# Second block in the wide order, shared sets mixed half in the first and half in the second block

## The reference

```python
xn = layernorm(x)                                   # no gain
s = silu(xn @ w_gate.T)                             # 2752 columns
idx = top_k(-abs(s), 1376)                          # per token: the smaller half by magnitude
s[idx] = 0
a = (s * (xn @ w_up.T)) @ w_down.T
h = relu(xn @ up_w) ** 2                            # 2048 columns
shared = h @ down_w
latent = xn @ fc1_w                                 # 512 columns
routed = (latent @ expert_w) * sum(top_k(xn @ gate_w, 2)) @ fc2_w
y = x + a + layernorm(shared + routed) * gamma + beta
```

## Time and profile before

| | |
|---|---|
| median of 3 runs | 2283.11 us (2279.87 to 2283.51) |
| the profiled execution | 2282.36 us, its span 2280.1 us |
| PE busy | 2263.9 us, 99% of the span, 10264 matmuls and transposes |
| VectorE (DVE) busy | 1327.3 us, 58% |
| GpSimd (POOL) busy | 939.2 us, 41% |
| ScalarE (ACT) busy | 751.3 us, 33% |
| granted TensorE clock | 1.00 over the span |
| DMA | 637.07 MB, mean 279 GB/s, engines busy 79.9% of the span |

### The profile page before, as it was taken

How to read it: one execution, slowest core, us unless ns; L and a number is a source line. 1 busy time by engine, 2 the same in 40 slices (tenths; PEclk the granted TensorE clock), 3 DMA queues, 4 the chain that set the end, 5 groups by cost and what they waited for, 6 DMA issues and landing times.

```text
span 2280.1 us, 27377 instructions
## 1 busy us (share of the span) xinstructions
PE 2263.9 (99%) x10264; PEld 1882.5 (83%) x10264; DVE 1327.3 (58%) x1712; ACT 751.3 (33%) x1173; POOL 939.2 (41%) x670
## 2 busy tenths in 40 slices
PE   8999999999999999999999999999999999999999
PEld 6888888888888888888888888888788888888877
DVE  4332678757334456937434446788943543888870
ACT  3233654133334325301114334623112432551310
POOL 5456557487444523044014461136403455043620
PEclk9999999999999999999999999999999999999999
DMA  6799999788888878887678887668677888676955
GB/s 257 278 389 395 354 366 354 264 341 299 292 297 280 273 278 312 295 292 289 213 233 296 272 278 284 213 228 288 239 251 248 268 283 309 216 231 226 333 186 177
DMA packets 229158, 637.07 MB, mean 279 GB/s; under 512 B 23712, under 2 KB 32928, under 8 KB 225952
## 3 DMA queue, kind: packets, MB, share of 16 engines
q1 hardware_dynamic: 229024, 635.30, 79.9%
HBM read 483.10 MB, written 152.11 MB: 279 GB/s over the span
## 4 chain that ended last, share of the span: by engine, by line
PE 92%; DVE 3%; DMA 2%; SPq 1%; POOL 1%; ACT 1%; issue 0%; DVEq 0%; ACTq 0%
PE bank L1330 30%; PE bank L1332 30%; PE bank L1331 30%; PE bank L1350 1%; DMA mixed_w<-mixes 1%; DVE prod L1925 1%; DMA split_w<-w 1%; PE bank L1341 1%; SPq L800 0%; POOL w L1061 0%; SPq L796 0%; DVE prod_t L2061 0%; DVEq L1491 0%; PE bank L1430 0%; PE bank L1431 0%
## 5 line engine op out<-in xcount | busy, mean ns | idle before, releaser
L1061 POOL TENSOR_TENSOR w<-raw,w 128x512 fp32r<-128x512 f32 (+1 forms) x196 | 282.3, 1447 | 195.0 <-ACT w L1107 194.6
L1066 POOL TENSOR_TENSOR w<-w 128x512 fp32r<-128x512 f32 x146 | 214.5, 1496 | 199.1 <-ACT w L1284 199.0
L1330 PE MATMUL bank<-w,prod_t 128*128 128x512 f32 x672 | 269.5, 401 | 3.0 <-DVE prod_t L2061 3.0
L1332 PE MATMUL bank<-w,prod_t 128*128 128x512 f32 x672 | 262.9, 391 | 0.0
L1331 PE MATMUL bank<-w,prod_t 128*128 128x512 f32 x672 | 261.9, 390 | 0.0
L1330 PE MATMUL bank<-w,tok 128*128 128x512 f32 (+1 forms) x664 | 252.8, 381 | 0.7 <-ACT mag L1218 0.5
L1331 PE MATMUL bank<-w,tok 128*128 128x512 f32 (+1 forms) x664 | 252.0, 380 | 0.0
L1332 PE MATMUL bank<-w,tok 128*128 128x512 f32 (+1 forms) x664 | 252.0, 379 | 0.0
L1330 PE MATMUL bank<-tok,w 128*128 128x512 f32 x640 | 249.0, 389 | 0.0
L1331 PE MATMUL bank<-tok,w 128*128 128x512 f32 x640 | 249.0, 389 | 0.0
L1332 PE MATMUL bank<-tok,w 128*128 128x512 f32 x640 | 249.0, 389 | 0.0
(11 more groups left out here) (222 smaller groups left out, 4633.7 us busy)
## 6 DMA issues: line engine op xcount, KB each, us to landing
w<-split_w SPq DMA_DIRECT2D x448, 512.0 KB, 4.5
split_w<-w SPq DMA_DIRECT2D x184, 512.0 KB, 6.2
w<-mixed_w SPq DMA_DIRECT2D x176, 256.0 KB, 3.2
w_more<-split_w SPq DMA_DIRECT2D x88, 512.0 KB, 5.1
w_more<-mixed_w SPq DMA_DIRECT2D x128, 256.0 KB, 3.7
rows<-x_dram SPq DMA_DIRECT2D x32, 512.0 KB, 5.0
mixed_w<-own SPq DMA_DIRECT2D x12, 1024.0 KB, 6.8
spilled_u<-prod SPq DMA_DIRECT2D x12, 1024.0 KB, 8.0
```

Source lines behind the costliest of these rows:

```text
L1061: pool.tensor_tensor(lo, words, hi, ALU.subtract).then_inc(lo_ready, 1)
L1066: pool.tensor_tensor(slot_of(g)[:, 1, :], slot_of(g)[:, 1, :].bitcast(F32), slot_of(g)[:, 0, :], ALU.subtract).then_inc(pool_lo, 1)
L1330: pe.matmul(out, left[0], right[0], start=first, stop=False)
L1332: return pe.matmul(out, left[1], right[0], start=False, stop=last)
```

## The change

`WIDE` becomes true for block 1, so its shared steps are computed as the pairs 5 and 6 in the wide order, 296 granules instead of 272. The sets that these pairs need are therefore mixed earlier. The four sets of pair 5 (`FIRST_SHARED`) are mixed in block 0, loaded from the granules 148, 158, 176 and 192, mixed seven and stored eight granules later, in a place of their own (`first_own`, over `below`); the first load waits for the first four masks. The four sets of pair 6 (`SECOND_SHARED`) are mixed in block 1, from the granules 149, 156, 163 and 170: two loads at each of two granules, the mix three and the store five behind, in `shared_own`. Two waits are added: the slots over `first_own` wait in block 1 for the first four stores, and ScalarE's `upper_early_sum` in block 1 for all eight, since it writes over `shared_own`. In all wide blocks the norms begin at out0+11 instead of out0+9 (three granules apart as before); the second token normalisation moves from out1+3 to out1+4, and the first two token loads from out0+18 and out0+21 to out0+20 and out1+1. The norm constants of block 1 are loaded where a wide block loads them, at 252. VectorE's operations for a set stay the same four.

```diff
--- before.py
+++ after.py
@@ -67,7 +67,7 @@
          (("shared", 0), ("shared", 1)), (("shared", 2), ("shared", 3))]
 
 FAST = [0, 5, 5, 5]
-WIDE = [False, False, True, True]
+WIDE = [False, True, True, True]
 SHARED_PAIRS = [5, 6]
 FIRST_PAIRS = 2
 UP_PAIR, SPILLED = 2, (3, 4)
@@ -262,12 +262,12 @@
         self.hidden_at = {end[("hidden", i)] + LAG + 1 + (1 if later and i > 1 else 2) * t: (i, t) for i in range(SC) for t in range(TILES)}
         if wide:
             self.read_hidden_at, self.hidden_at = {}, {}
-        self.norm_at = [out0 + (9 if wide else 6) + (3 if later else 5) * t for t in range(TILES)]
-        self.tokens_at = [out1 + 1, out1 + 3] if wide else [out0 + 20, out0 + 21] if later else [out1 + 2, out1 + 4]
+        self.norm_at = [out0 + (11 if wide else 6) + (3 if later else 5) * t for t in range(TILES)]
+        self.tokens_at = [out1 + 1, out1 + 4] if wide else [out0 + 20, out0 + 21] if later else [out1 + 2, out1 + 4]
         self.tokens_at += [out1 + 10, out1 + 14]
         self.turn_tokens_at = {out1 + TURN_AFTER[t] + LAG: t for t in range(TILES)}
         self.residual_load = [ups + 2, ups + 3, self.norm_at[0] + 3, self.norm_at[1] + 3]
-        self.tokens_load = [out0 + 18, out0 + 21] if wide else [out0 + 14, out0 + 15] if later else [self.norm_at[2] + 3, self.norm_at[3] + 3]
+        self.tokens_load = [out0 + 20, out1 + 1] if wide else [out0 + 14, out0 + 15] if later else [self.norm_at[2] + 3, self.norm_at[3] + 3]
         self.tokens_load += [out1 + 7, out1 + 11]
 
 
@@ -445,10 +445,12 @@
 
 
 SHARED_SETS = range(SHARED_PAIRS[0] * HALF, (SHARED_PAIRS[1] + 1) * HALF)
-SHARED_FROM = {n: 158 + 7 * i for i, n in enumerate(SHARED_SETS)}
-SHARED_LOADS = {at + i: (n, i) for n, at in SHARED_FROM.items() for i in range(4)}
-SHARED_AT = {at + 5: n for n, at in SHARED_FROM.items()}
-SHARED_STORES = {at + 6: n for n, at in SHARED_FROM.items()}
+FIRST_SHARED, SECOND_SHARED = SHARED_SETS[:HALF], SHARED_SETS[HALF:]
+SHARED_FROM = [dict(zip(FIRST_SHARED, (148, 158, 176, 192))), dict(zip(SECOND_SHARED, (149, 156, 163, 170)))]
+SHARED_LOADS = [{at + i: [(n, i)] for n, at in SHARED_FROM[0].items() for i in range(4)},
+                {at + i: [(n, 2 * i), (n, 2 * i + 1)] for n, at in SHARED_FROM[1].items() for i in range(2)}]
+SHARED_AT = [{at + 7: n for n, at in SHARED_FROM[0].items()}, {at + 3: n for n, at in SHARED_FROM[1].items()}]
+SHARED_STORES = [{at + 8: n for n, at in SHARED_FROM[0].items()}, {at + 5: n for n, at in SHARED_FROM[1].items()}]
 
 
 MIX_PLACE = [0, 3, 2, 1]
@@ -628,6 +630,7 @@
 
         w_more = over("w_more", [P, EXTRA, 2, N], F32R, more_at)
         own = over("own", [P, 4, N], F32, more_at)
+        first_own = over("first_own", [P, 4, N], F32, more_at + 2 * HID * 4)
         junk_at = nc.sbuf_base - GK * P * 4
         junk_v = over("junk_v", [P, GK, P], BF16, junk_at)
         junk_s = over("junk_s", [P, GK, P], U8, junk_at + GK * P * 2)
@@ -775,6 +778,10 @@
 
             return raw_more[:, i, :]
 
+        def shared_place(n):
+
+            return first_own if n in FIRST_SHARED else shared_own
+
         def results_of(name):
 
             kind, c = name
@@ -834,16 +841,18 @@
             def load_shared_mix(n, i):
 
                 p, k = n // HALF, n % HALF
-                if n > SHARED_SETS[0]:
+                if n == FIRST_SHARED[0]:
+                    sp.wait_ge(masked, TILES)
+                elif n != SECOND_SHARED[0]:
                     sp.wait_ge(shared_stored, 16 * (n - SHARED_SETS[0]))
                 else:
                     sp.wait_ge(bank_filled, filled(1, ("fast", FAST[1] - 1, len(PRODUCTS) - 1, 1)))
                 src, width = words_of((PAIRS[p][i // 2], k + i % 2 * HALF))
-                sp.dma_start(shared_own[:, i, :], src).then_inc(shared_loaded, 16)
+                sp.dma_start(shared_place(n)[:, i, :], src).then_inc(shared_loaded, 16)
 
             def store_shared_mix(n):
                 sp.wait_ge(shared_mixes, 4 * (n - SHARED_SETS[0]) + 4)
-                sp.dma_start(mixed_w[n].rearrange("i p n -> p i n"), shared_own[:, :, :]).then_inc(shared_stored, 16)
+                sp.dma_start(mixed_w[n].rearrange("i p n -> p i n"), shared_place(n)[:, :, :]).then_inc(shared_stored, 16)
 
             def load_norm(b):
 
@@ -868,6 +877,8 @@
                 slot_free(sp, g)
                 if SLOT[g] >= RING and m < PHASE[b, 0] + RING + EXTRA:
                     sp.wait_ge(apply_step, b * 4 * TILES)
+                    if b == 1:
+                        sp.wait_ge(shared_stored, 16 * len(FIRST_SHARED))
                 for n, p in enumerate(SHARED_PAIRS):
                     if WIDE[b] and SLOT[g] >= RING and m in range(PHASE[b, p], PHASE[b, p] + RING + EXTRA):
                         if n == 0:
@@ -929,10 +940,11 @@
                     load_own_mix(*OWN_LOADS[m])
                 if b == 0 and m in OWN_STORES:
                     store_own_mix(OWN_STORES[m])
-                if b == 1 and m in SHARED_LOADS:
-                    load_shared_mix(*SHARED_LOADS[m])
-                if b == 1 and m in SHARED_STORES:
-                    store_shared_mix(SHARED_STORES[m])
+                if b < 2:
+                    for n, i in SHARED_LOADS[b].get(m, []):
+                        load_shared_mix(n, i)
+                    if m in SHARED_STORES[b]:
+                        store_shared_mix(SHARED_STORES[b][m])
                 if m == (plan.norm_load if b else FIRST_NORM_LOAD):
                     load_norm(b)
                 if b:
@@ -1187,6 +1199,8 @@
             def upper_early_sum(b, n):
 
                 act.wait_ge(unit_summed, shared_round(b, n) * UNIT_SUMS + 1)
+                if b == 1 and n == 0:
+                    act.wait_ge(shared_stored, 16 * len(SHARED_SETS))
                 act.activation(unit_sums_r[:, SUM_SLOT["S3"][0], :, :], unit_sums[:, EARLY_RAW, :, :],
                                ACT.Copy).then_inc(unit_sum_hi, 1)
 
@@ -1565,7 +1579,7 @@
 
             def mix_shared(n):
 
-                b11, b21, b12, b22 = (shared_own[:, i, :] for i in range(4))
+                b11, b21, b12, b22 = (shared_place(n)[:, i, :] for i in range(4))
                 at = 4 * (n - SHARED_SETS[0])
                 dve.wait_ge(shared_loaded, 64 * (n - SHARED_SETS[0] + 1))
                 dve.tensor_tensor(b11, b12, b11, ALU.subtract).then_inc(shared_mixes, 1)
@@ -1989,8 +2003,8 @@
                         dve.wait_ge(mixed_hi, MIXED[g])
                         dve.tensor_tensor(slot_of(g)[:, 1, :], slot_of(g)[:, 1, :].bitcast(F32), slot_of(g)[:, 0, :],
                                           ALU.subtract).then_inc(vector_lo, 1)
-                    if b == 1 and m in SHARED_AT:
-                        mix_shared(SHARED_AT[m])
+                    if b < 2 and m in SHARED_AT[b]:
+                        mix_shared(SHARED_AT[b][m])
                     if m in plan.units_at:
                         make_units(b, *plan.units_at[m])
                     if m in plan.lower_at:
```

## The result

The changed kernel takes 2288.43 us, median of 15 runs (2284.73 to 2291.79), the kernel before 2281.75 beside it (15 runs, 2279.87 to 2286.73): ratio 1.0027, interval 1.002 to 1.0034. So it is slower by 4.6 to 7.8 us. The forecast was 2282.5, no change; the time lies inside its range, near the 2291 of rival (b). The profiled execution took 2288.73 us with a span of 2286.9, 6.8 more than the span before.

A forecast was written before the change was run, and what follows sets the result against it. PE, busy nearly the whole span, was taken as the bound: matmul and transpose count plus stalls. Terms +2.7 +0.1 -4.1 +0.6 = -0.7 on the profiled 2282.36 gave 2281.7, or 2282.5 as median; range 2273 to 2292.

The forecast's parts named there:

- rival (b): Whole kernel slower: second-block chain later than walked, stage stall 16, clock 2.2, first block 4, giving 2291 us; chance 0.19.
- The direct gain: Second block: 48 matmuls fewer, 10.9 us; priced whole by the third block as 8.2 us, 557.29 to 549.06.
- The norm shift: out0 of blocks 2 and 3: norms two granules later save 2.05 us in each, 4.1 in all.
- the mixes in the search: Second block, VectorE's search chain: mixes and their load waits delay PE's operands, a stall of 10.4 us.
- the stall of the stage: Second block, pair 5: PE stalls 10.4 us in total because VectorE's chain is late; bounds 7 and 16.
- the walk: Second block: VectorE's chain timed step by step from granule 148's start, putting A12 at 108.3 us, wanted at 97.9.
- Step 5: Second block, a search step in VectorE's chain, put at 88.8 us from granule 148's start.
- First block: +2.7: Block 0, granules 155 to 164: four more sets' loads and stores delay raw loads, costing 2.7 us; bounds 0.5 and 6.
- Sets 22 and 23: nothing: Block 0: these two sets cost nothing, falling where raw halves have 5 to 9 us of lead.
- Covered, by 1 us: Wide blocks: banks free by 1680.7, first token turned about 1681.9, so the later second token row costs nothing.
- rival (c): Norm shift does not pay: second token row late, stall moves from out0 to out1, 2288.6 us; chance 0.10.
- Clock: +0.6: Second block: stalls of 2 to 5 us may halve PE's clock once, costing 0.6 us; bounds 0 and 4.4.

The follow-up runs named there:

- two_places: Changed kernel with pair 6's sets in two alternating places, loaded ahead and mixed where VectorE stood idle; 2271.18 us, ratio 0.9957 to the kernel before.
- norms_only: Kernel before with only the out0 norms, token normalisations and token loads of the wide blocks moved; 2277.11 us, ratio 0.9985.
- places_only: Changed kernel with pair 6's sets in two alternating places, loads at 149, 152, 163, 168, mixes unmoved; 2281.15 us, ratio 0.9995 to the kernel before.
- first_mix_later: Changed kernel with the mix of set 24 at granule 157 instead of 152, still one place; 2287.43 us, ratio 1.0027 to the kernel before.
- sets_in_out1: Changed kernel with block 0's sets 22 and 23 loaded from 186 and 200, mixed at 195 and 207; 2293.18 us, ratio 1.0055 to the kernel before.
- no_mix_work: Changed kernel without VectorE's mix operations for sets 24 to 27, loads, stores and waits kept; 2284.57 us, ratio 1.0017 to the kernel before.
- combined: two_places with block 0's sets 22 and 23 loaded, mixed and stored later, second token row at out1; 2266.85 us, ratio 0.9938 to the kernel before.

## Why the prediction was wrong

**What was right.** The direct gain: the bare wide second block as 547.0 (546.9 in two_places). The norm shift as -4.1 (-4.0 in norms_only). That the mixes in the search turn the gain of the second block into a stall through VectorE, not through PE's or the memory's load; the first wait and the start of the chain up to 32 us within 0.4 us.

**The term that failed: the stall of the stage, 10.4 us, measured 16.9** (563.95 less 547.0). The step that failed is the walk's landing time of a store. It had mix 25 at 33.4, which leaves 5.0 us for the store of set 24, the median of the earlier trace rows. The store landed after 9.2 us, and mix 25 came 4.5 us late: 4.2 by the store, 0.3 by what was late before. places_only, which takes this wait away, gains 5.8. Step 5's slow operation adds 2.2, the walk had 1 us too much elsewhere, and the last 0.8 us lie behind A12 (PE began its product 0.65 us behind VectorE, the walk had it there at once). I took the median for a place where the queue holds two spills, and that choice turned the sign. In the seven kernels with the changed second block the store of set 24, issued among the spills, took 5.8 to 12.3 us; the eight stores of the kernel before took 5.0 to 5.9. That the spills are what slows it fits, but no run took them away.

Rival (b) came near in time, 2291, in part by luck. Its bound of 16 us for the stall stood on loads landing near 7.8 us and on a mix of 6.8. The loads of the sets 24 to 27 landed within 6.6 us in the kernel after, and the mixes there took 0.68 us an operation.

**Where PE stands.** The prediction named ScalarE's and VectorE's operands. The first wait (5.2) is for VectorE's units; the largest (6.2) is for GpSimd's half of the weights at granule 184. These slots lie over the search's scratch, SP may load them only when the last count is done (931.05), so they are late by the same chain. A price by A12 alone still came out right, since A12 was ready at the same moment. The other kernels bear it out: A12 was late against 97.1 by 16.9, 16.6, 16.3, 12.4 and 11.3 us (after, first_mix_later, sets_in_out1, no_mix_work, places_only), and block 1 was longer than 547.0 by 16.9, 16.5, 16.3, 12.3 and 11.1.

**First block: +2.7, measured 3.6, or 4.5 from granule 40 on.** Size inside the bounds, place wrong. The raw loads at 155 to 164 had no lateness. "Sets 22 and 23: nothing" was the wrong sentence: it weighed only SP's raw loads and not VectorE's queue, where set 22 stands ahead of halves of turned products that PE reads at once. It waits 3.9 us there and works 6.4, and sets_in_out1 and combined gave those 4.1 us back. Another 0.7 us at granule 174 stayed in both, and no run names their cause.

**Norm shift.** Right alone, -2.7 in the kernel after, because the second token row was late once. "Covered, by 1 us" was 0.7; rival (c) happened with 1.7 us of its 6.1, in one block.

**Clock: +0.6, measured about 0.** The clock did fall to half, twice, so the wait-then-slow mechanism was right, but both times PE had another wait ahead in the same stage. I had added the term to the stall, and it must be weighed against what is late next; this is worked out from the traces, for no run changes the clock alone. Where nothing is, it costs: in sets_in_out1 the wait of 4.1 us before granule 201 was the last of its stretch, the granted clock between 600 and 603 us was 0.70, and granule 201 took 4.44 us for 2.72. (Columns as in the earlier trace rows.)

```profile
598.00:600.00 2.00, 1.91 (x5) 1.57 (x6) 1.02 (x2) 2.00 (x5) 2.00 (x3) 0.60 1.05 417
600.00:603.00 3.00, 3.00 (x11) 2.30 (x11) 0.36 (x1) 0.17 (x1) 1.75 (x2) 0.70 1.03 400
```

**Sum.** -0.8 (head, not of the change) + 3.6 + 6.7 - 0.35 - 2.3 = +6.8 against the -0.7 worked out. The one mis-sized term, 6.5 us too low, is most of the 7.5 us between them. The Trainium skill (DMA: Bandwidth & Descriptors, Rules for kernel authors), issue early and wait late, agrees with two_places; but first_mix_later waited later and gained nothing, since with one place the load itself couldn't be issued early.

## What to carry to other kernels

A buffer that is loaded, worked on and stored in a round has a period of its own: price the round (load landing, wait for the engine, work, store landing at that place of the queue) before the work, and try a second place before you move the work. Put side work into the idle gaps that the timeline of the same stage already shows; there 10.8 us of it cost nothing, while ahead of queued work 4 operations cost 4 us. Where a store waits for a mix, list it well behind the mix, for what is queued behind it may be a row that three other engines wait for.

## What the runs showed of the hardware

- VectorE and GpSimd slow each other. Where GpSimd works on tensors as well, a mix operation takes 1.5 to 1.8 us instead of 0.69 (rows of set 22 above), and GpSimd's own operations in that stretch 1.73 instead of 1.29, both at the same pace of 1.7 us. The Trainium skill (SBUF — State Buffer, SBUF: two separate sides) has an exclusive lock on a port pair that the two share, one blocked while the other's operation runs; the equal pace agrees. By turns alone it would be 1.85 us, an estimate from their starts when each is alone (0.60 and 1.25 us apart); the measured 1.7 is a little less, and no run here explains that. GpSimd in the same stretch:

```profile
534.26 1.29 POOL L1073 TENSOR_TENSOR w<-raw,w 128x512 fp32r<-128x512 f32 x1
535.51 1.73 POOL L1104 TENSOR_TENSOR prod<-prod,mag 128x512 f32<-128x512 f32 x1
537.20 1.74 POOL L1073 TENSOR_TENSOR w<-raw,w 128x512 fp32r<-128x512 f32 x1
```

- The granted clock fell to its lower level (1.2 GHz) toward the end of PE's waits of 6.2 and 5.2 us and, in sets_in_out1, right behind the one of 4.1 us in mid-kernel. It stayed at 1.00 (2.4 GHz) behind the wait of 2.1 us before granule 168 in no_mix_work and behind those of 1.0 to 1.4 us in out0 of block 0.
- The landing of one and the same kind of store or load swings from kernel to kernel: 5.8, 9.2 and 12.3 us for the 1 MB store of set 24 among the spills in three kernels, 4.2 or 6.7 us for a token row at the same granule of two kernels.
